# Second attention: who scales and masks the keys, and who releases the fetch of the next ones

## The reference

```python
xq = q.reshape(b, s, 8, 4, 16)
xk = k.reshape(b, t, 8, 16)
xv = v.reshape(b, t, 8, 16)
scores = jnp.einsum('bsgrd,btgd->bgrst', xq, xk) / math.sqrt(16)
scores = scores + mask
probs = jax.nn.softmax(scores, axis=-1)
out = jnp.einsum('bgrst,btgd->bsgrd', probs, xv)
```

## Time and profile before

| what | value |
|---|---|
| runs of the kernel before | 1215.52, 1219.99, 1218.9 us; median 1218.9 us |
| the profiled execution's own time | 1212.91 us |
| its span, first to last instruction | 1211.2 us |
| mean granted clock of TensorE | 0.953 of 2.4 GHz |

### The profile page before, as it was taken

The page is one execution under the profiler, slowest core; times in us unless marked ns, Lnnn a source line. Parts: engine busy times, 40 slices in busy tenths (PEclk is TensorE's granted clock), DMA queues, the critical chain, the costliest instruction groups (busy, mean ns, idle before and its releaser), DMA issues.

```text
span 1211.2 us, 23648 instructions
## 1 busy us (share of the span) xinstructions
PE 1114.7 (92%) x9380; PEld 597.2 (49%) x9380; DVE 691.5 (57%) x1221; ACT 473.4 (39%) x829; POOL 420.9 (35%) x369
## 2 busy tenths in 40 slices
PE   7878996998998889999999999999989889999996
PEld 3444553776675444444444444444556544444442
DVE  6777674687787674535312521522289933656465
ACT  4566672675654553322111211211257622322231
POOL 2245475888882230000280060000043400325163
PEclk8887886899999999999999999999999989999998
DMA  7000000111120220310010000000000000000001
GB/s 238 2 2 4 22 10 14 41 43 36 38 77 4 64 64 22 101 52 34 19 61 20 1 20 32 0 1 1 0 12 9 2 1 1 12 24 17 17 27 44
DMA packets 29011, 35.91 MB, mean 30 GB/s; under 512 B 5882, under 2 KB 20499, under 8 KB 28788
## 3 DMA queue, kind: packets, MB, share of 16 engines
q1 hardware_dynamic: 27506, 34.53, 8.9%
q10 hardware_dynamic: 1410, 0.06, 0.1%
HBM read 30.24 MB, written 4.19 MB: 28 GB/s over the span
## 4 chain that ended last, share of the span: by engine, by line
PE 64%; DVE 12%; issue 3%; ACT 3%; POOL 0%; DVEq 0%; POOLq 0%; ACTq 0%
PE p_up L116 10%; PE p_up L117 10%; PE p_up L118 10%; PE p_y L116 8%; PE p_y L118 8%; PE p_y L117 8%; PE p_y L1527 3%; DVE e_den L2234 2%; PE p_up L1492 1%; PE p_up L1515 1%; DVE wd_lo L103 1%; PE p_up L110 1%; DVE st L188 1%; PE p_up L1497 1%; PE p_y L110 1%
## 5 line engine op out<-in xcount | busy, mean ns | idle before, releaser
L1926 DVE TENSOR_TENSOR d_h_low<-d_hf,d_h_high 128x512 f16<-128x512 f32 (+1 forms) x40 | 27.8, 695 | 205.1 <-ACT d_h_high L2015 205.1
L116 PE MATMUL p_up<-d_xt_high,wd_hi 128*128 128x512 f16 (+1 forms) x352 | 133.4, 379 | 2.9 <-PE p_y L118 1.5
L117 PE MATMUL p_up<-d_xt_low,wd_hi 128*128 128x512 f16 (+1 forms) x352 | 133.4, 379 | 0.0
L118 PE MATMUL p_up<-d_xt_high,wd_lo 128*128 128x512 f16 (+1 forms) x352 | 133.4, 379 | 0.0
L170 ACT ACTIVATE d_sg<-p_up 128x512 f32<-128x512 f32 (+1 forms) x40 | 23.7, 594 | 212.8 <-PE p_up L118 212.8
L116 PE MATMUL p_y<-wd_hi,d_h_high 128*128 128x512 f16 (+1 forms) x272 | 103.1, 379 | 0.0
L118 PE MATMUL p_y<-wd_hi,d_h_low 128*128 128x512 f16 (+1 forms) x272 | 103.1, 379 | 0.0
L117 PE MATMUL p_y<-wd_lo,d_h_high 128*128 128x512 f16 (+1 forms) x272 | 103.1, 379 | 0.0
L138 POOL TENSOR_SCALAR wd_raw<-wd_raw 128x1156 f32<-128x1156 f32 x8 | 25.1, 3137 | 207.1 <-DVE d_h_low L1926 207.1
L435 POOL TENSOR_TENSOR a_pt_low<-a_ex,a_pt_high 128x1024 f16<-128x1024 f32 x32 | 68.0, 2126 | 80.3 <-ACT a_pt_high L924 80.2
L2196 POOL TENSOR_TENSOR wd_hi<-wd_hi,e_den 128x1024 f32<-128x1024 f32 x16 | 30.5, 1907 | 147.3 <-DVE e_den L2236 147.3
(11 more groups left out here) (340 smaller groups left out, 2938.9 us busy)
## 6 DMA issues: line engine op xcount, KB each, us to landing
wd_raw<-in_w_d SPq DMA_DIRECT2D x16, 616.0 KB, 3.7
wd_raw<-in_w_f SPq DMA_DIRECT2D x8, 578.0 KB, 3.8
X<-in_x SPq DMA_DIRECT2D x4, 1024.0 KB, 12.3
wd_lo<-in_ctx_t SPq DMA_DIRECT2D x128, 32.0 KB
out_x<-wd_raw SPq DMA_DIRECT2D x16, 256.0 KB, 2.0
wd_lo<-in_ctx SPq DMA_DIRECT2D x32, 64.0 KB, 2.4
wd_raw<-in_w_c SPq DMA_DIRECT2D x1, 1096.0 KB, 12.4
wd_hi<-in_Wo SPq DMA_DIRECT2D x1, 1024.0 KB
```

Source lines behind the costliest of these rows:

```text
L116: nc.tensor.matmul(ps, st[0], mv[0], start=start, stop=False)
L117: nc.tensor.matmul(ps, st[0], mv[1], start=False, stop=False)
L118: return nc.tensor.matmul(ps, st[1], mv[0], start=False, stop=stop)
L1926: nc.vector.tensor_tensor(hid[1][0:n, d % NH, :], value, hid[0][0:n, d % NH, :], ALU.subtract).then_inc(h_ready, 1)
```

## The change

GpSimd's scaling into `ks` goes, and ScalarE makes it: one half at the end of each step n, half 0 of tile (n-1)/2+3 at odd n, behind `high_keys` of that tile, and half 1 of tile n/2+2 at even n, behind `high_x`. Before each, ScalarE waits until GpSimd has done the subtraction that read `ks` last. GpSimd's wait for the key fetch goes, since `ks_ready` and `bd_high` now stand for it. SP's `fetch` waits for ScalarE's second high part and second scaling of tile t-2 in place of GpSimd's second subtraction.

```diff
                 def fetch(c, i):
                     t, b = TC * c + i, i % 2
 
-                    sp.wait_ge(bd_ready, 2 * t + 1)
+                    sp.wait_ge(bd_high, 2 * t - 2)
+                    sp.wait_ge(ks_ready, 2 * t - 2)
...
                 pool.sem_inc(bd_ready, 5)
-                pool.sem_inc(ks_ready, 2)
-
                 def tile(c, i, fresh):
                     t, b = TC * c + i, i % 2
 
-                    if fresh:
-                        wait_apart(pool, kt_in[b], 128 * (TC // 2 * c + i // 2), held.apart)
                     for h in range(2):
                         wait_apart(pool, vb_ready if h == 0 else bd_ready, VB * t + 2 * VB if h == 0 else 2 * t + 4,
                                    held.apart)
-                        nc.gpsimd.tensor_scalar(ks, kt[:, b, :, :].rearrange("p k n -> p (k n)"),
-                                                held.mask_bs[:, h:h + 1], None, ALU.mult).then_inc(ks_ready, 1)
                         wait_apart(pool, ks_ready, 2 * t + h + 1, held.apart)
...
+                def keys(t, h):
+                    act.wait_ge(bd_ready, 2 * t + 3 + h)
+                    nc.scalar.activation(ks, kt[:, t % 2, :, :].rearrange("p k n -> p (k n)"), ACT.Copy,
+                                         scale=held.mask_bs[:, h:h + 1]).then_inc(ks_ready, 1)
+
...
                 act.sem_inc(bd_high, 2)
+                act.sem_inc(ks_ready, 2)
                 high_x(0)
                 high_x(1)
                 high_keys(1)
+                keys(1, 0)
                 high_keys(2)
...
                             high_x(n // 2 + 2)
                         if n % 2 and n // 2 + 3 < NT:
                             high_keys(n // 2 + 3)
+                    if n % 2 and n // 2 + 3 < NT:
+                        keys(n // 2 + 3, 0)
+                    if n % 2 == 0 and n // 2 + 2 < NT:
+                        keys(n // 2 + 2, 1)
```

## The result

| what | before | after |
|---|---|---|
| runs shown with the result | 1215.52 to 1220.3 us, median 1219.45 (4 runs) | 1199.36 to 1207.63 us, median 1200.91 (4 runs) |
| the profiled execution's own time | 1212.91 us | 1207.63 us |
| its span | 1211.2 us | 1205.9 us |
| its mean granted clock | 0.953 | 0.945 |
| row maxima of unit 4 to unit 30 | 133.49 us | 121.35 us |

The change makes the kernel faster: the ratio of the times is 0.9871, with a 95% interval of 0.9832 to 0.991. The medians stand 18.5 us apart and the two profiled executions only 5.3 us. The last row of the table is the one that holds still from execution to execution.

The account below looks back on a forecast made before the run. GpSimd's tile of 10.08 us against TensorE and VectorE's 9.35 was taken as the bound. Waits and the clock behind them, 11.94 us, go and nothing is added: 1218.9 - 12 = 1207 us, range 1203 to 1214.

Parts of the forecast that it names:

- What bound the kernel: Second attention: GpSimd loses 0.73 us of its lead a tile, used up at tile 8; tiles then exceed 9.35 us.
- The sum: Second attention, eight late tiles: direct waits on GpSimd and the lower clock behind them go, 11.94 us, taken as 12.
- The single long addition at 348.93: VectorE's residual addition before the change, 1.67 us, 0.98 too long; counted in the 11.94, may or may not recur.
- ScalarE's scaling: ScalarE's new copy at each step's end: 0.7 us, fitting idles of 0.92 and 1.15 us, at no cost.
- The added wait: In `keys`, ScalarE waits for GpSimd's last subtraction: 2.1 us in reserve, 0.2 with the statistics, priced at 0.
- SP's part: SP's key fetch, issued in 4.59 us and released earlier, stays hidden 11.5 us ahead of its use: 0.
- VectorE beside GpSimd: VectorE's residual addition falls beside GpSimd's casts of the values: priced at 0, otherwise 0.98 us a tile.
- The clock doesn't come back: Rival: in the second attention only TensorE's idle goes, together 6 us, giving 1213 us; chance 0.15.
- The meeting is locked in: Rival: a GpSimd subtraction of keys starts with each residual addition, tiles last 10.33 us, 1220 us; chance 0.09.
- ScalarE stands at GpSimd's subtraction: Rival: in `keys`, half 1, GpSimd over 2.1 us late; further delay w costs w - 0.2 a tile, 1228 us; chance 0.07.

Follow-up runs that it names:

- half of the move: The changed kernel, but only half 0 of each tile's scaling is ScalarE's and half 1 is GpSimd's again; median 1205.49 us, ratio 0.9892.
- the old release: The changed kernel, but SP's fetch of keys waits for GpSimd's second subtraction as before; median 1203.08 us, ratio 0.9876.

## Why the prediction was right

**What bound the kernel.** Right. GpSimd used up a lead, then TensorE stood. With GpSimd's tile at 269.06 - 262.35 = 6.7 us (changed) or about 8.2 (half of the move) the eight late tiles take 9.3 to 9.7 us.

**The sum.** I priced 11.94 us by the row maxima and rounded to 12; the traces show 12.14 and 12.17 up to unit 30. The single long addition at 348.93 didn't come again. Unit 30's maxima came at 353.63 where I had 351.9, because unit 4's came 1.97 us later: the clock rose later at the attention's start in this execution.

My sum had no term for what follows unit 30, and there some of the gain is given back. From unit 30's maxima to the last residual addition pass 17.45 and 17.48 us in the two traces of the kernel before, but 18.58 and 19.26 in those of the changed kernel and 19.45 with the old release. TensorE stands about 2 us twice there in both kernels; from 8 to 13 us behind unit 30's maxima its granted clock is 1.00 before and 0.61 to 0.68 in these three. So from unit 4 to its last addition the attention gains 10.2 to 11.0 us. Why the clock falls sooner there is open.

The forecast of 1207 us lies above the median of 1200.91, and so does the range I had stated, by 2 us; the mean of the twelve runs of the changed kernel, 1203.6, lies at its lower edge. I took 12 us off a median of three runs, and the medians of one and the same kernel move by 3.6 us. So the mechanism and its price in the attention came out, and the whole time only just. The means of all runs differ by 14.2 us, with a standard error of 1.2 from their scatter, and the attention gives 10 to 11 of them. Where the other 3 to 4 come from is open: the kept traces don't hold them, for the spans of the two of before (1211.2 and 1213.3 us) and of the three above (1205.9, 1198.9 and 1202.7 us) differ by 9.8 us on average. Before unit 4 the executions scatter anyway: over the traces of all runs its maxima come between 226.08 and 234.43 us.

**ScalarE's scaling.** I took 0.7 us and it is 0.71 to 0.73. The idle left is 0.31 and 0.53 us where I had 0.2 and 0.45, since instructions of one queue overlap by 0.1 us. The price of 0 holds, and it has an edge: 0.61 us more a step costs 2.8 us over the attention, 1.6 of them in the two tiles where ScalarE also waits for GpSimd.

**The added wait.** The reserve was 2.1 us by my sum and is 1.6: the first subtraction ends at 267.90 + 1.16 = 269.06, ScalarE asks at 261.36 + 9.34 = 270.70. I had missed that GpSimd needs 0.37 us, not 0.2, from the end of the values to the next subtraction, and that the casts lengthen by 0.35. In the tile behind the statistics I had 0.2 us in reserve; it was 0.22 late, absorbed. There the reserve is really at its end: with GpSimd 1 us later ScalarE stood 0.67 and 0.86 us, and these two tiles are among the three longest in each of the four runs in which GpSimd or ScalarE was slowed.

**SP's part.** Hidden, as said; undoing it changes nothing that the runs show.

**VectorE beside GpSimd.** I put the addition into the casts at a price of 0. It does fall there, and lasts 0.79 us in place of 0.69. The tile isn't longer for it than the 9.35 I worked with (9.34), but where the addition takes 0.69, tiles last 9.31: the price is 0.03 us a tile.

**The rivals.** *The clock doesn't come back*: wrong. With the idle gone the clock is 1.00 from 286 to 340 us. *The meeting is locked in*: it didn't happen, since the phase was as I worked it out, but the mechanism is real. I had priced it at 0.98 us in each tile; forced, it cost 0.5 in ten of thirteen, because the addition started 0.43 us after the subtraction and not with it. The three tiles in which they start together cost 1.6 to 2.3 us each, but ScalarE's wait is in them too; only both together left 1.2 us of 12. *ScalarE stands at GpSimd's subtraction*: it didn't happen, and forced it makes the attention slower than before. My price of w - 0.2 a tile lacked the clock, which made three tiles cost most of it.

By the Trainium skill (GPSIMD Engine Reference, section Specifications), which has VectorE instructions with two SBUF inputs contend with GpSimd, each meeting should cost. The runs agree for GpSimd's instructions that read two tiles: where the addition started behind such a subtraction, it ended 0.54 or 0.55 us after it. For those with one input they agree only in small part: casts and scalings cost the addition 0 to 0.24 us. At most it was 0.93 us in place of 0.69, in the second trace of the kernel before, where it started 0.30 us behind a scaling of 1.56 us.

Who starts first matters as well, and I hadn't seen it in the trace of before. There the addition of 272.42 started 0.04 us ahead of a subtraction and took its 0.69 us, and GpSimd paid, with 1.67 us in place of 1.16:

```profile
272.46 1.67 POOL L1299 TENSOR_TENSOR wd_lo<-wd_lo 128x512 f16<-128x512 f32 x1 [0.28 <-ACT wd_lo L1435]
```

## What to carry to other kernels

An engine that is busy for a third of the span can bound a stage: look at its instructions in time, and whether the only idle between them is its own. Then shortening its loop below the next engine's gives the whole gain, and half of the move gave nearly as much here. Before an engine's work gets a fixed phase to another's, lay its two-input instructions beside those of VectorE: a meeting that drifted through once may come in every tile.

## What the runs showed that I had not expected

TensorE's clock made waits dear in an uneven way. With GpSimd late and meeting the addition, TensorE stood 0.34 us in each of ten tiles, for 0.5 us more a tile, and 2.05 us in two places in each of the two behind statistics, for 2.3 us more; its clock stayed at 1.00 from 225 to 360 us. With ScalarE made to wait, one idle of 0.58 us was followed by a lower clock (0.73 from 255 to 260 us, 0.93 from 260 to 265) and its tile lasted 11.64 us, 2.3 more than 9.34; two later idles of the same 0.58 us left the clock at 1.00 and their tiles at 9.96. The two idles of 2.3 us cost 5.1 and 3.9 us. So a wait cost between one and four times itself, and which it was can't be told from its length here: about 2 us of it cost 2.3 us with the clock at 1.00 in one run and 3.9 to 5.1 us with a lower one in another.
